# AdaLN, linear attention and a top-2 mixture of experts on one core: expert tiles of two 128-row halves, and all split expert weights kept on chip

## The reference, cut to what matters

```python
h = _layernorm(x) * (1 + ca) + sa
x = x + ga * attn(h)                       # phi(q), phi(k), causal, divided by sum(z * q)
h = _layernorm(x) * (1 + cb) + sb
normed = _layernorm(h, rn_g, rn_b)
logits = normed @ router_w.T + router_b
top_w, top_idx = top_k(logits, 2); top_w = softmax(top_w)
for e in range(8):
    t = _layernorm(h, ln_g[e], ln_b[e])
    t = gelu(t @ w1[e] + b1[e], approximate=False)      # 256 -> 1024
    out = out + combine[..., e] * (t @ w2[e] + b2[e])   # 1024 -> 256
x = x + gb * out
```

## Time and profile before

| | |
|---|---|
| median of 3 runs | 1220.99 us (1219.15 to 1221.44) |
| profiled execution: its own time, its span | 1220.36 us, 1218.6 us |
| busy: PE, DVE, ACT, POOL | 85%, 75%, 45%, 48% |
| granted TensorE clock, mean | 0.901 |
| data moved by DMA | 172.01 MB |

### The profile page before, as it was taken

The page is one execution under the profiler, slowest core; times in us unless marked ns, Lnnn a source line. Parts: engine busy times, 40 slices in busy tenths (PEclk is TensorE's granted clock), DMA queues, the critical chain, the costliest instruction groups (busy, mean ns, idle before and its releaser), DMA issues.

```text
span 1218.6 us, 34018 instructions
## 1 busy us (share of the span) xinstructions
PE 1031.0 (85%) x8284; PEld 836.8 (69%) x8285; DVE 908.2 (75%) x3005; ACT 549.2 (45%) x1122; POOL 588.7 (48%) x487
## 2 busy tenths in 40 slices
PE   5768676878754059999999998999999999999996
PEld 2435453545443048787888887888888888888885
DVE  4588999999975337676777777777778777787774
ACT  2577767767732023333444333443434444443332
POOL 1112656555657715444454454445554545455553
PEclk8789788886865579999999999999999999999998
DMA  4456565757564356677555766566655666666663
GB/s 155 151 173 217 198 248 177 267 183 249 166 216 180 125 144 153 123 169 162 90 101 98 178 104 159 96 106 109 102 94 98 98 97 103 104 104 104 105 98 41
DMA packets 164887, 172.01 MB, mean 141 GB/s; under 512 B 91772, under 2 KB 138120, under 8 KB 160744
## 3 DMA queue, kind: packets, MB, share of 16 engines
q1 hardware_dynamic: 130664, 114.75, 34.0%
q0 software_dynamic: 34176, 56.72, 25.7%
HBM read 228.66 MB, written 63.69 MB: 240 GB/s over the span
## 4 chain that ended last, share of the span: by engine, by line
PE 59%; issue 15%; DVE 10%; POOL 8%; DMA 3%; SPq 2%; ACT 1%; DVEq 0%; POOLq 0%; ACTq 0%
PE banks L1275 29%; PE banks L1287 28%; POOL lists L489 5%; POOL rs L482 3%; DMA rowbuf<-lists 2%; DVE st L705 2%; DVE store L879 1%; DVE ix L907 1%; DVE store L855 1%; PE banks L1108 1%; SPq L381 1%; DMA store<-in_L_wmod 1%; DVE dl L905 0%; DVE mv L710 0%; SPq L371 0%
## 5 line engine op out<-in xcount | busy, mean ns | idle before, releaser
L1275 PE MATMUL banks<-nhl,store 128*128 128x256 bf16 x3408 | 468.4, 274 | 58.6 <-DMA nhl<-xhl 45.9
L1287 PE MATMUL banks<-store 128*128 x3408 | 466.8, 273 | 0.0
L675 ACT ACTIVATE gf<-banks,b1t 128x256 f32<-128x256 f32 x568 | 267.3, 474 | 442.0 <-PE banks L1275 409.1
L1275 PEld LDWEIGHTS banks<-nhl,store 128*128 x3408 | 330.8, 98 | 108.8 <-issue 69.1
L525 POOL DMA_INDIRECT out<-rowbuf,ydst x142 | 229.3, 1615 | 338.5 <-DVE rowbuf L1057 278.1
L1287 PEld LDWEIGHTS banks<-store 128*128 128x128 bf16 x3408 | 332.1, 98 | 42.4
L1065 DVE CAST store<-gf 128x256 bf16<-128x256 f32 x568 | 173.7, 306 | 174.9 <-ACT gf L675 128.0
L1067 DVE TENSOR_TENSOR store<-gf,store 128x256 bf16<-128x256 f32 x568 | 242.1, 426 | 19.5
L489 POOL DMA_INDIRECT lists<-nrm,slot x128 | 137.6, 1075 | 110.6 <-DVE nrm L939 75.3
L516 POOL DMA_INDIRECT store<-y_rows,ygb x142 | 149.3, 1051 | 68.9 <-issue 42.0
L482 POOL TENSOR_TENSOR rs<-ve,mhalf 128x12 f32<-128x12 f32 (+2 forms) x20 | 38.9, 1943 | 97.6 <-DVE ve L716 97.5
(11 more groups left out here) (204 smaller groups left out, 999.8 us busy)
## 6 DMA issues: line engine op xcount, KB each, us to landing
store<-wsplit SPq DMA_DIRECT2D x142, 1024.0 KB, 11.2
rowbuf<-lists SPq DMA_DIRECT2D x71, 264.0 KB
store<-in_L_ffn_w SPq DMA_DIRECT2D x16, 1024.0 KB, 5.8
wsplit<-store SPq DMA_DIRECT2D x16, 1024.0 KB, 4.9
b2t<-in_L_ffn_b SPq DMA_DIRECT2D x71, 128.0 KB
store<-in_L_attn_x SPq DMA_DIRECT2D x16, 512.0 KB
out<-store SPq DMA_DIRECT2D x16, 512.0 KB
csB<-mod_rows SPq DMA_DIRECT2D x16, 256.0 KB
```

Of the source, the lines that this page charges most:

```text
L675: a.activation(gf[:, c % 2, :], MM[c % 2][:, 0:TOK], ACT.Gelu, bias=b1t[:, r, c:c + 1]).then_inc(gf_s, 1)
L1275: last = t.matmul(MM[c % 2][:, 0:TOK], w, nhl[:, r, m, :], start=n == 0, stop=n == 5)
L1287: last = t.matmul(ACC[r][h][:, 0:D], g[:, c, h * P:(h + 1) * P], w, start=c == 0 and n == 0, stop=c == NI - 1 and n == 2)
```

## The change

A tile is still 256 rows but two halves of 128, each with an expert of its own. The table has one entry for each of `HALVES` = 136 halves, so there are 68 tiles. All eight experts' split weights are on chip before the fourth tile: experts 0 to 3 in the place of the residual rows, 4 and 5 in the split buffers, 6 and 7 in the place of `nrm`, `pt`, `hT` and others, which now lie behind each other in `store`. Experts 0 and 1 are loaded by SP during phase one (after steps 9 and 13), 4, 5, 2 and 3 at its end, 6 and 7 after the loads of the second tile; the ring, its table rows and `weights_ahead` are gone. `first` makes six matmuls for each half, of 128 columns. Gelu is done for each half, rows and biases are loaded for each half. The table's code on DVE is shorter, and it is written so that independent operations stand between one and the wait for it. One fill scatter an expert is left of two. Since a token may now stand in both halves of a tile, the two output scatters are one after the other, with the gathers of the tile after next between them. The cores of the edits:

```diff
-TILES = (2 * NTOK + E * (TOK - 1)) // TOK
+HALVES = -(-((2 * NTOK + E * (P - 1)) // P) // TH) * TH
+TILES = HALVES // TH
...
-        wring = store[:, NB * NC * D - 2 * NI * D:].bitcast(bf16).rearrange("p (s n) -> p s n", s=3)
-        wbuf = wring[:, 1:3, :]
+        wall = store[:, 0:E * SLOT].bitcast(bf16).rearrange("p (e n) -> p e n", e=E)
+        wbuf = wall[:, NB * NC * D // SLOT:AFTER // SLOT, :]
...
+            def resident(e):
+
+                for at in (0, 4096):
+                    sp.dma_start(wall[:, e, at:at + 4096], wsplit_d[e, :, at:at + 4096]).then_inc(got_we[e // TH], 16)
...
+            for i in range(NB):
+                step(i, i // 2, i % 2)
+                if i in (9, 13):
+                    resident_in_rows(i // NC - 2)
...
+            resident(4)
+            resident(5)
+            resident_in_rows(2)
+            resident_in_rows(3)
...
-            rows_load(0, 0)
-            rows_load(1, 1)
+            for j in range(2):
+                rows_load(j, j)
+            flip(0, 0)
             bias_load(0, 0)
-            flip(0, 0)
-            sp.wait_ge(x2_out, 16 * NB)
-            for j in range(1, E):
+            tile_loads(1, 1)
+            resident(6)
+            resident(7)
...
-                    a.activation(gf[:, c % 2, :], MM[c % 2][:, 0:TOK], ACT.Gelu, bias=b1t[:, r, c:c + 1]).then_inc(gf_s, 1)
+                    for h in range(TH):
+                        last = a.activation(gf[:, c % 2, h * P:(h + 1) * P], MM[c % 2][:, h * P:(h + 1) * P], ACT.Gelu, bias=b1t[:, r, h, c:c + 1])
+                    last.then_inc(gf_s, 1)
...
-                in_reg = [t.alloc_register(f"slot{loads[0]}_{m}") for m in range(n)]
-                t.reg_load(in_reg, table[0:1, 3, ds(j, n)])
-                return [ds(t.snap(reg, donate=True, min_val=0, max_val=2), 1) for reg in in_reg]
+                in_reg = [t.alloc_register(f"slot{loads[0]}_{m}") for m in range(TH * n)]
+                t.reg_load(in_reg, table[0:1, 0, ds(TH * j, TH * n)])
+                at = [ds(t.snap(reg, donate=True, min_val=0, max_val=E - 1), 1) for reg in in_reg]
+                return [at[TH * m:TH * m + TH] for m in range(n)]
...
-                n = 0
-                for k in range(NK):
-                    head = wring[:, s, k * I + c * P:k * I + (c + 1) * P]
-                    rest = wring[:, s, 2048 + k * I + c * P:2048 + k * I + (c + 1) * P]
-                    for w, m in ((head, k), (head, NK + k), (rest, k)):
-                        last = t.matmul(MM[c % 2][:, 0:TOK], w, nhl[:, r, m, :], start=n == 0, stop=n == 5)
-                        n += 1
+                for h in range(TH):
+                    n = 0
+                    for k in range(NK):
+                        head = wall[:, s[h], k * I + c * P:k * I + (c + 1) * P]
+                        rest = wall[:, s[h], 2048 + k * I + c * P:2048 + k * I + (c + 1) * P]
+                        for w, m in ((head, k), (head, NK + k), (rest, k)):
+                            last = t.matmul(MM[c % 2][:, h * P:(h + 1) * P], w, nhl[:, r, m, h * P:(h + 1) * P], start=n == 0, stop=n == 5)
+                            n += 1
...
-                head = wring[:, s, 4096 + c * D:4096 + (c + 1) * D]
-                rest = wring[:, s, 6144 + c * D:6144 + (c + 1) * D]
                 for h in range(TH):
+                    head = wall[:, s[h], 4096 + c * D:4096 + (c + 1) * D]
+                    rest = wall[:, s[h], 6144 + c * D:6144 + (c + 1) * D]
```

More of the change, by code:

```diff
@@ L162, in adaln_moe_kernel @@
+        tab_e = sb("tab_e", [P, HALVES]); tab_r, tab_d = (store[:, free + E * MAXT + n * HALVES:free + E * MAXT + (n + 1) * HALVES] for n in range(2 * E, 2 * E + 2)); hop = sb("hop", [P, E])
+        table = sb("table", [P, 3, HALVES], i32)
         banks = ctx.enter_context(nc.psum_tensor("banks", [P, 8, 512], f32))
@@ L368, in _, with entry @@
             sp.wait_ge(tab_s, 1)
+            def entry(k, row, top):
+                return nc.sync.value_load(table[0:1, row, ds(k, 1)], min_val=0, max_val=top)
             def rows_load(j, r):
-                row = nc.sync.value_load(table[0:1, 1, ds(j, 1)], min_val=0, max_val=DUMMY)
+                row = [entry(TH * j + h, 1, DUMMY) for h in range(TH)]
                 wait_past(sp, nl_s, j - 1)
                 wait_past(sp, yw_s, j - 1)
-                if isinstance(j, int) and j < E:
+                if isinstance(j, int) and j < E // TH:
@@ L974, in _ @@
-            tchain(v.tensor_tensor(need[:, :, :], count[:, :].unsqueeze(2).to_broadcast([P, E, MAXT]), steps[:, :, :], ALU.is_gt))
+            have(is_large)
+            moved = put(v.tensor_tensor(fillf[:, :], shift[:, :], large[:, :], ALU.mult))
+            have(needs)
+            counted = put(v.tensor_reduce(ntile[:, :], need[:, :, :], axis=AX.X, op=ALU.add))
+            have(moved)
+            filled = put(v.tensor_tensor(fillf[:, :], fillf[:, :], fill[:, :], ALU.add))
+            have(counted)
@@ new lines, in _ @@
+            ends = put(v.tensor_tensor_scan(tend[:, :], onesf[:, 0:E], ntile[:, :], 0.0, ALU.mult, ALU.add))
+            have(filled)
+            v.tensor_tensor(filli[:, :], fillf[:, :], base[:, :], ALU.add).then_inc(filli_s, 1)
+            have(ends)
+            starts = put(v.tensor_tensor(tstart[:, :], tend[:, :], ntile[:, :], ALU.subtract))
+            passed = put(v.tensor_tensor(ge[:, :, :], tid[:, :].unsqueeze(2).to_broadcast([P, HALVES, E]), tend[:, :].unsqueeze(1).to_broadcast([P, HALVES, E]), ALU.is_ge))
@@ L975, in _ @@
+            have(starts)
+            deltas = put(v.scalar_tensor_tensor(delta[:, :], tstart[:, :], float(P), offs[:, :], ALU.mult, ALU.subtract))
+            have(passed)
+            found = put(v.tensor_reduce(tab_e[:, :], ge[:, :, :], axis=AX.X, op=ALU.add))
             dve.wait_ge(b1v_ps, 1)
             v.tensor_tensor(b1f[:, :, :].rearrange("p e i -> p (e i)"), vecs[:, VEC_B1:VEC_G], V[:, 0:E * NI], ALU.add).then_inc(b1f_s, 1)
-            tchain(v.tensor_reduce(ntile[:, :], need[:, :, :], axis=AX.X, op=ALU.add))
@@ new lines, in _ @@
+            put(v.tensor_tensor(hop[:, 0:E - 1], delta[:, 1:E], delta[:, 0:E - 1], ALU.subtract))
+            hops = put(v.memset(hop[:, E - 1:E], 0.0))
+            have(found)
+            bounded = put(v.tensor_scalar(tab_e[:, :], tab_e[:, :], float(E - 1), None, ALU.min))
+            have(hops)
+            hopped = put(v.tensor_tensor(gs[:, :, :], ge[:, :, :], hop[:, :].unsqueeze(1).to_broadcast([P, HALVES, E]), ALU.mult))
+            have(bounded)
+            put(v.tensor_copy(table[:, 0, :], tab_e[:, :]))
@@ new lines, in _ @@
+            have(hopped)
+            summed = put(v.tensor_reduce(tab_r[:, :], gs[:, :, :], axis=AX.X, op=ALU.add))
+            put(v.memset(table[:, 2, 0:2 * TH], 1))
+            put(v.tensor_tensor(table[:, 2, 2 * TH:HALVES], tab_e[:, 2 * TH:HALVES], tab_e[:, 0:HALVES - 2 * TH], ALU.not_equal))
+            have(summed)
+            have(put(v.scalar_tensor_tensor(tab_r[:, :], tid[:, :], float(P), tab_r[:, :], ALU.mult, ALU.subtract)))
+            have(put(v.tensor_scalar(tab_d[:, :], tab_r[:, :], -1.0, float(DUMMY), ALU.mult, ALU.add)))
@@ L1012, in _ @@
+            have(put(v.tensor_tensor(tab_d[:, :], tab_d[:, :], ge[:, :, E - 1], ALU.mult)))
+            v.tensor_tensor(table[:, 1, :], tab_r[:, :], tab_d[:, :], ALU.add).then_inc(tab_s, 1)
+            have(tc[0])
             dve.wait_ge(tab_s, 1)
@@ L1314, in _ @@
             hold(pe, "pe")
[L1315 to L1316 removed]
+            used_sets = sets_from(0, 5)
+            for j in range(5):
                 tile(j, j // 2, j % 2, j == 0, used_sets[j - 1], used_sets[j])
[L1318 removed]
+            with t.Fori(2, (TILES - 1) // 2 - 1) as h:
                 used_sets = sets_from(2 * h, 3)
```

260 lines of the change are left out of this document (109 added, 151 removed).

## The result

The changed kernel takes **1435.07 us** (median of three runs, 1435.03 to 1436.88), the kernel before 1220.99. The ratio is 1.176, with a 95% interval of 1.174 to 1.179. The forecast was 1427, with a range from 1340 to 1505.

The account below looks back on a forecast made before the run. PE's sequencer, with twelve address operations a chunk, was to bound the changed kernel: 1220.4 + 207 (tiles) + 1.8 (scatters at the end) - 2 (between the phases) = 1427 us, range 1340 to 1505.

Parts of the forecast that it names:

- part 3: PE's sequencer in the tiles: twelve address operations at 0.127 us plus 0.08 make 1.6 us a chunk, over the array's 1.33.
- (a): Faster rival: PE's sequencer stays hidden at no more than 0.087 us a distance, array the bound, 1183 us; chance 6%.
- (b): Rival: a price in between for PE's address distance, 0.09 to 0.115 us, giving 1190 to 1350 us; chance 7%.
- part 2: PE array's work in a tile: narrow matmuls at 0.056 us, 1.33 us a chunk, 10.6 us a tile.
- rival (c): Narrow matmuls of `first` save nothing on PE: 1.96 us a chunk, 15.7 a tile, 1530 us; chance 6%.
- rival d: PE's clock falls to 1.2 GHz because the array idles: 21.2 us a tile, over 1850 us; chance 3%.
- part 4: Other engines: work hidden behind PE; output scatters in a row fit inside 14.45 us a tile, +1.8 us at the end.
- the stretch between the phases: From the table's end to the first transposes, with a shorter table but SP still waiting: -2 us, between -10 and +10.
- the sum for the tiles: PE's tiles: 867 us in the loop, 62.5 first five, 41 last three, with small terms 975 for 768, +207.
- one such stall: PE waiting for row loads behind weights: at most one stall stays, for the 4 MB of experts 6 and 7.
- Its top: Top of the tiles' loop on PE's sequencer: 1.7 us before, 0.7 more for three more words loaded, 2.4 us.
- The last sign of being wrong on record: PE waiting in the tiles for ACT, DVE or a transposed row, meaning a wait priced at nothing has come up.

Follow-up runs that it names:

- Run 3: Kernel before, nothing of the change, with twelve address operations a chunk for its twelve wide matmuls instead of six: 1476.2 us, 1.20 times the kernel before.
- run 1: Changed kernel with the weights' place as constants on PE, no address operations or table loads, all 18 matmuls kept: 1258.5 us, kernel before 1226.3.
- run 7: Changed kernel without address operations, plain transfers replacing the transposing ones in the loop, on the second chip: 1180.5 us.
- run 6: Kernel before with each gelu of 256 columns as two of 128, on the second chip: 1204.7 us against 1198.8, ratio 1.0049.
- run 12: Kernel before with all eight experts' weights resident, whole tiles of one expert kept, on the first chip: 1210.05 us against 1220.8, ratio 0.9911.
- run 8: Changed kernel without address operations, one gelu of 256 columns a chunk instead of two, on the second chip: 1190.5 us.
- run 2: Changed kernel with both halves on the first half's expert, six addresses a chunk worked out once, all 18 matmuls kept: 1294.8 us.

## Why the prediction was right

By place, from the profiled executions, all in us: the first matmul came 14.5 us earlier (424.1 for 438.6); from there to the end of the last group 997.4 us for 768.2, +229.2; behind it 13.7 for 11.8, +1.9. The sum is +216.6, and 1436.9 - 1220.4 = 216.5.

**The sequencer (part 3) was the bound, at the price read.** 0.127 us a distance was read from eleven of them. Summed over the sequencer's rows of the whole loop, the time from each address operation to the next row is 0.127 on average, and the 192 of a pair of tiles take 24.4 us for the 24.4 forecast. Run 3 has 24.5 for its 192, without the change, and run 1 takes them away. Rivals (a) and (b) needed distances under 0.115. The step by which one sees it in the profile of before is the earlier trace rows: an engine's sequencer has a pace of its own, and it can be read where it catches up.

**The array's work (part 2) was right**: 0.056 was taken for a narrow matmul, and 0.056 was found near 437 and again in run 7 over 350 us, so rival (c) is out. The Trainium skill (TensorE: Matmul & The Clock Gate, "Back-to-back issue gap") gives about 81 ns for such a pair of weight load and matmul. By that the tile of run 7 would be an estimated 13.0 us; it was 10.60. The measurement decides: where nothing stands between these matmuls, 81 ns is too much.

**The clock (rival d)** stayed at 1.00 in the loop, though a chunk takes 0.3 us more than the array's work in it.

**The scatters (part 4)** fit, as forecast, "but not by much inside 10.6": in run 7, at 10.60 us a tile, PE was busy all the time, though DVE waited 33 times for a landed scatter (its waits from 800 to 1150):

```profile
DVE ydst L1068 <- DMA out<-rowbuf,ydst: 44.9, 33, 2.2
```

At the end the kernel is +1.9 longer for the 1.8 forecast: in the changed kernel's timeline of POOL the last two start 4.24 us apart, for 1.87 in the earlier trace rows:

```profile
1424.42 1.55 POOL L542 DMA_INDIRECT out<-rowbuf,ydst  x1 [2.80 <-DMA out<-rowbuf,ydst]
1428.66 1.55 POOL L542 DMA_INDIRECT out<-rowbuf,ydst  x1 [2.70 <-DMA out<-rowbuf,ydst]
```

**Two terms were mis-sized, and they partly cancel**: -12.5 us against +22, which leaves the 10 between 1427 and 1436.9. That the total came out so near is in part luck. The first is the stretch between the phases, put at -2 us (between -10 and +10); it was -14.5, outside those bounds. Here the kernel before was slow rather than the changed one fast, as the table loads of SP's line 381 show: first the kernel before, between 412 and 436, then the same line of run 6, which differs from it on ACT alone, on the second chip:

```profile
L381 SPq TENSOR_LOAD <-table x2: 688/696/703, 426.0 to 430.2; - x2
```

```profile
L381 SPq TENSOR_LOAD <-table x2: 268/269/270, 414.0 to 414.6; - x2
```

The same instructions take 2.6 times as long. SP is not alone in it: DVE's operations for the table, from 395.8 to 411.3 in the kernel before, are the same in run 6 and last there from 395.6 to 404.9. In run 6 the first matmul comes at 421.45, even earlier than in the changed kernel. So a good part of the 23 us of the earlier trace rows goes with the chip, and I priced all of it as the kernel's. It is not the chip alone: single loads of 0.64 to 0.68 us stand in run 6 too, at 419 and 424, and the change itself, and the resident weights alone, get rid of the slow stretch on the first chip, where the first matmul is at 436.6 in run 3, at 419.9 in run 1 and at 419.6 in run 12. Which part of them does so, and what slows both engines, is open.

The second mis-sized term is the sum for the tiles, +207 on record, +229 measured. The loop is 8 us over the forecast, 1 in 100. The last tiles are 1 us over it. The first five are 13 us over it (77.9 us from 424.1 to 502.0, for 64.7 with the wait for the first gelu). Part of that is the "one such stall" of part 4, named there and given no price in the sum. The waits of the changed kernel from 420 to 500:

```profile
ACT xhl L687 <- DMA rowbuf<-lists: 14.1, 2, 9.3
PE banks L1302 <- ACT gf L697: 10.6, 5, 7.2
```

Inside the loop, too, two errors cancel, by luck. Its top was read too dear: the load of six words was put at 0.77 + 0.7 = 1.5 us and took 0.82, so the top takes 1.7 us a pair and not 2.4 (the words don't set the time of a load: the three of four words behind the loop take 0.35, 1.08 and 0.34). What makes up for most of it is a wait that part 4 had at nothing. ACT stands in the changed kernel too, for 3.1 us in one tile of a pair and 2.7 in the other:

```profile
956.28 0.62 ACT L697 ACTIVATE gf<-banks,b1t 128x128 f32<-128x128 f32 x2 [1.31 <-PE banks L1302]
959.99 1.14 ACT L697 ACTIVATE gf<-banks,b1t 128x128 f32<-128x128 f32 x4 [3.09 <-PE banks L1302]
```

The longer one reaches the sequencer. In its rows the address operation that waits for a gelu comes late once a pair, 0.04 us behind the end of such a gelu; by 0.6 us on average, and in a third of the pairs another 0.5 us stands ahead of it with no releaser to be seen. PE itself stands for a gelu once a pair (waits from 502.0 to 1377.5):

```profile
PE banks L1302 <- ACT gf L697: 11.5, 30, 0.5
```

So the sequencer's own work fills some 28.4 of the 29.17 us, and the wait for ACT is about 2%. The last sign of being wrong on record, PE waiting in the tiles for ACT, did come, at this small size. No run takes this wait away by itself.

**What the change would be without its addresses**: on the first chip 1.03 to 1.04 times the kernel before, on the second 0.985 (run 7, less the transposes) to 0.993 (run 8, less a gelu). So the gain for which it stands, three tiles less, is there in the array's work, but it needs addresses that cost the sequencer no more than 1.33 us a chunk, and even then a chip may not give it.

## What to carry to other kernels

An address that comes out of a register has a price on the sequencer, here 0.124 us (the usual distance) to 0.127 us (the mean) for each different one, and it is hidden only while the matmuls behind it take longer. Before cutting matmuls in two, or giving halves a source of their own, add up the different addresses in a group and compare with the array's time for it; where the same address serves several matmuls, work it out once (run 2: -140 us). And compare variants side by side on one chip, the unchanged one among them: two explanations seemed to be shown here by runs 7 and 8, and both fell on the chip where the trouble was.

## What the runs showed of the hardware that I had not expected

- Between the two chips the same kernel before differs by 2% (1220.8 and 1198.8 us). Most of that has a place, the stretch between the phases, where single SP instructions take 0.70 us for 0.27 and the first matmul comes at 438.6 and not at 421.45 (run 6 stands in for the kernel before on the second chip).
- Kernels without address operations differ more: 1262.7 and 1258.6 us on one chip, 1180.5 and 1190.5 on the other, with ACT standing for 2.0 to 3.5 us in nearly every tile on the first, its matmuls long done. The kernel before hasn't this stand in the loop (one of 1.9 us from 800 to 1150).
- The pace of the address operations doesn't depend on the array's clock: 28.98 and 29.00 us for two tiles in run 3, with and without a piece at the lower level.
- A table load of six words takes 0.82 us, one of three 0.77: hardly more. Loads of four words take 0.34 to 1.08.
